# Two more attention steps get their sums over keys from a pair of fp16 matmuls instead of one fp32 matmul

## What is computed

```
attn = softmax(q k^T * scale)                 # over 666 keys
x = x + (attn v) @ Wout
x = x + sum_e score_e * (relu(LN(x) @ W1_e + b1_e) @ W2_e + b2_e)
```

## Time and profile before

| | us |
|---|---|
| runs | 343.05, 342.17, 342.32 |
| median | 342.32 |
| profiled execution | 342.39 |
| its span (first to last instruction) | 340.7 |
| PE busy | 331.6 (97%) |
| POOL busy | 287.5 (84%) |
| DVE busy | 274.1 (80%) |
| ACT busy | 214.5 (63%) |

### The profile page before, as it was taken

The page is one execution under the profiler, slowest core; times in us unless marked ns, Lnnn a source line. Parts: engine busy times, 40 slices in busy tenths (PEclk is TensorE's granted clock), DMA queues, the critical chain, the costliest instruction groups (busy, mean ns, idle before and its releaser), DMA issues.

```text
span 340.7 us, 5981 instructions
## 1 busy us (share of the span) xinstructions
PE 331.6 (97%) x2193; PEld 220.5 (65%) x2193; DVE 274.1 (80%) x416; ACT 214.5 (63%) x303; POOL 287.5 (84%) x186
## 2 busy tenths in 40 slices
PE   7899999999999999999999999999999999999993
PEld 7676666574847565665757474756694548888782
DVE  5988667988899899999988798979728786499476
ACT  2464668584948476675858494857622745587980
POOL 4629999999999999999999999999993999488540
PEclk9999999999999999999999999999999999999998
DMA  4640000000010000000000000000000007000611
GB/s 128 194 118 0 2 0 4 0 17 0 2 31 16 17 2 0 3 1 2 15 2 15 18 0 17 0 2 1 2 0 3 0 0 228 22 0 2 189 63 62
DMA packets 9049, 10.03 MB, mean 29 GB/s; under 512 B 1015, under 2 KB 6061, under 8 KB 9021
## 3 DMA queue, kind: packets, MB, share of 16 engines
q1 hardware_dynamic: 8725, 9.52, 9.3%
q10 hardware_dynamic: 296, 0.13, 0.1%
HBM read 9.09 MB, written 0.56 MB: 28 GB/s over the span
## 4 chain that ended last, share of the span: by engine, by line
PE 90%; ACT 3%; DVE 3%; POOL 1%; issue 1%; DMA 1%; ACTq 0%; DVEq 0%
PE xo L476 25%; PE sc L456 21%; PE sc L462 6%; PE sc L382 5%; PE sc L384 4%; PE sc L383 4%; PE mx L413 3%; PE xo L413 3%; PE mx L564 2%; PE xo L564 2%; PE xo L485 2%; PE mx L383 1%; PE mx L382 1%; PE mx L384 1%; POOL relu_lo L1275 1%
## 5 line engine op out<-in xcount | busy, mean ns | idle before, releaser
L1297 POOL TENSOR_TENSOR psum_acc<-psum_acc,probs 111x1024 f32<-111x1024 f32 x64 | 164.0, 2562 | 6.9
L768 ACT ACTIVATE probs<-sc 111x1024 f32<-111x1024 f32 x96 | 98.2, 1027 | 18.5 <-PE sc L462 11.9
L476 PE MATMUL xo<-probs,v_sb 111*64 111x512 f32 x384 | 88.0, 596 | 0.0
L456 PE MATMUL sc<-q_pair,k_pair 64*111 64x512 f32 x576 | 86.0, 402 | 0.8 <-ACT v_sb L758 0.4
L456 PEld LDWEIGHTS sc<-q_pair,k_pair 64*111 64x111 f32 x576 | 44.6, 171 | 28.4 <-issue 11.5
L995 DVE RECIPROCAL recips<-recips 128x128 f32<-128x128 f32 x64 | 54.0, 903 | 0.0
L476 PEld LDWEIGHTS xo<-probs,v_sb 111*64 111x64 f32 x384 | 26.3, 137 | 42.7 <-issue 39.4
L961 DVE TENSOR_REDUCE part_max<-mx 128x2 f32<-128x888 f32 x32 | 34.7, 1083 | 20.5 <-PE mx L413 19.0
L1297 POOL TENSOR_TENSOR psum_acc<-probs 111x1024 f32<-111x1024 f32 x16 | 39.3, 2458 | 7.8 <-ACT probs L768 7.6
L784 ACT COPY recips<-xo 128x512 f32<-128x512 f32 x16 | 9.4, 587 | 57.5 <-PE xo L485 48.8
L462 PE MATMUL sc<-max_row,ones_r 64*111 64x512 f32 x192 | 38.3, 390 | 0.0
(11 more groups left out here) (238 smaller groups left out, 619.8 us busy)
## 6 DMA issues: line engine op xcount, KB each, us to landing
spread<-score_rows SPq DMA_DIRECT2D x16, 256.0 KB, 5.7
w_raw<-in_L_ffn_W SPq DMA_DIRECT2D x8, 128.0 KB, 2.1
x_tok<-in_x SPq DMA_DIRECT2D x2, 256.0 KB, 3.2
wv_raw<-in_L_xattn_Wkv SPq DMA_DIRECT2D x4, 128.0 KB, 2.9
wout_sb<-in_L_xattn_Wout SPq DMA_DIRECT2D x1, 512.0 KB
wqk_raw<-in_L_xattn_Wq SPq DMA_DIRECT2D x7, 64.0 KB, 2.0
wqk_raw<-in_L_xattn_Wkv SPq DMA_DIRECT2D x7, 64.0 KB, 2.1
out<-x_tok SPq DMA_DIRECT2D x1, 256.0 KB, 2.0
```

The source lines that it names most:

```text
L456: pe.matmul(sc[0:KP, kt % 2, h, :], k_pair[r, s % QKB, k_part, at], q_pair[r, s % QKB, q_part, :], start=(k_part + q_part == 0), stop=False)
L476: mm = pe.matmul(o_ps[h * HD:(h + 1) * HD, :], v_sb[0:KP, s // 2 % 2, kt, at:at + HD], probs[0:KP, e % RING, h, :], start=(kt == 0), stop= ...
L768: act.activation(probs[0:KP, e % RING, :, :], sc[0:KP, kt % 2, :, :], ACT.Exp).then_inc(exp_done, 1)
L1297: pool.tensor_tensor(psum_acc[0:KP, s % 2, :, :], first, probs[0:KP, e % RING, :, :], ALU.add) \
```

## The change

`HALVED` goes from `STEPS - 3` to `STEPS - 1`, so `total(13)` and `total(14)` take the two fp16 parts too; `total(15)` stays fp32. The places of the `total` calls on PE are the same as before, which the rewritten condition keeps. ACT gets `sum_high(13)` behind the exponents of step 14 and `sum_high(14)` behind that step's last `w2_high`. DVE gets `sum_low(13)` as the last call of its loop, behind `spread_max(15)`, and `sum_low(14)` behind `norm_x1(0)`, ahead of the `reciprocal(12)` calls. The reciprocals keep their places. `gather(15, 1)` now waits on `acc_lo_done` in place of `sum_ready`.

```diff
-HALVED = STEPS - 3
+HALVED = STEPS - 1
@@ PE, step s
                 turn_max(s + 1)
-                if s > HALVED:
-                    total(s - 1)
                 for kt in range(KT):
-                    if kt == SUM_AT and 1 <= s <= HALVED:
+                    if kt == (SUM_AT if s < STEPS - 2 else 0) and s >= 1:
                         if s == 1:
                             pe.wait_ge(kv_ready, 3)
                         total(s - 1)
@@ ACT, step s
-                if 2 <= s <= HALVED:
+                if 2 <= s < STEPS - 1:
                     sum_high(s - 1)
@@
                 for e in W2_HI_AT.get(s, ()):
                     w2_high(e)
+                if s == STEPS - 2:
+                    sum_high(s)
@@ DVE, step s
-                if 1 <= s <= HALVED:
+                if s >= 1:
                     sum_low(s - 1)
-                if 2 <= s <= HALVED:
+                if 2 <= s < STEPS - 2:
                     for c in range(RC):
                         reciprocal(s - 2, c)
@@ DVE, behind the loop
             x1_and_moments(0, x1_ps[0])
             norm_x1(0)
+            sum_low(STEPS - 2)
             for c in range(RC):
                 reciprocal(STEPS - 4, c)
```

## The result

| | before | after |
|---|---|---|
| median, us | 342.99 (342.17 to 343.05, 5 runs) | 346.67 (346.42 to 347.23, 5 runs) |
| profiled execution | 342.39 | 346.42 |
| its span | 340.7 | 344.7 |

The ratio is 1.0121, 95% interval 1.0108 to 1.0135, which is 4.1 us (3.7 to 4.6). In the two profiled executions the difference is 4.03 us. The two medians lie only 3.7 us apart, since the runs of before are of two kinds, near 342.2 and near 343.0, and its median is one of the upper ones. The forecast was 345.3, that is +3.0; the rival in which the clock falls was put at 346.6.

The account below looks back on a forecast made before the run. PE, busy for 97% of the span, was taken to bound the kernel: +3.1 (stall) - 0.96 (two totals) + 0.9 (second wait) = +3.0 us, forecast 345.3 us, range 343.9 to 346.8.

Parts of the forecast that it names:

- the rival in which the clock falls: `pv(14)` runs partly at 1.2 GHz after the stall, 2.2 us added, PE +4.3: 346.6 us; chance 0.14.
- The stall: PE waits ahead of `total(13)` for `sum_low(13)`, which stands behind `spread_max(15)` on DVE: 3.1 us.
- The length of `sum_low`: `sum_low(13)` waits for the end of the `gather` under way, then takes 1.08 us, ending at 258.62.
- DVE's and POOL's lateness: Both `sum_low` calls delay `reciprocal(12)` by 3.26 us; POOL's row follows, its last `gather` ending at 282.55.
- The second wait: PE waits ahead of `total(15)` for POOL's late last `gather`: 0.9 us.
- The clock: Granted clock stays at 1.00 in `pv(14)` behind the stall; no time added.
- two totals: `total(13)` and `total(14)` on PE each get 0.48 us shorter in fp16: -0.96 us.

Follow-up runs that it names:

- ingap: Changed kernel with `sum_low(13)` moved ahead of `spread_max(15)` on DVE; ratio 1.006 to the kernel before, median 344.45 us.
- w2late: Changed kernel with POOL's `w2_low(0)` moved from ahead of step 14's last `gather` to behind `rstd_x1(0)`; ratio 1.0112 to before, median 346.49 us.
- awake: Changed kernel with 12 unread identity matmuls on PE between `turn_max(15)` and `total(13)`; ratio 1.0107 to the kernel before.
- ingap_awake: Changed kernel with `sum_low(13)` ahead of `spread_max(15)` and 7 unread identity matmuls ahead of `total(15)`; ratio 1.0028 to before, median 343.33 us.
- gap13_swap: Changed kernel with only `total(13)` split, `sum_low(13)` ahead of `spread_max(15)`, `bias_term(0)` ahead of `total(15)`; ratio 1.0013 to before, median 342.63 us.
- only13: Changed kernel with only `total(13)` split, `total(14)` left fp32; ratio 1.0135 to the kernel before, median 347.51 us.
- only14: Changed kernel with only `total(14)` split, `total(13)` left fp32; ratio 1.0062 to the kernel before, median 344.53 us.

## Why the prediction was right or wrong

**The stall: right.** Forecast: `sum_low(13)` from 256.43 to 258.62, `total(13)` at 258.8, `pv(14)` 2.6 us late. Measured: 256.46 to 258.66, 258.71, 2.57. That DVE's wide gap is of no use, since the call stands behind the instruction that PE releases last, is shown by ingap, where the stall is gone with that order alone.

**The length of `sum_low`: right.** It ends 1.08 to 1.09 us behind the end of the `gather`, at four places of it (kernel after, w2late, ingap, and the call in the earlier trace rows). The rule of the Trainium skill ("SBUF — State Buffer", section "Who interferes with whom") holds here: whoever begins first holds the interface for its whole instruction. In ingap it shows in the other direction too, in the `gather` of 3.15 us begun during `sum_low`.

**DVE's and POOL's lateness: right, but hidden.** `reciprocal(12)` came 3.28 us late (forecast 3.26). The second wait, put at 0.9 us, was 0.16 in the kernel after, since PE had lost 1.67 us elsewhere by then. With the clock kept up (awake) it was 0.75.

**The clock: wrong, and this is the step that failed.** The forecast had "the granted clock 1.00 in `pv(14)`" and gave the fall a chance of 0.14. The sum had no term for it. By profile or mean clock it fell in 9 of 9 runs of the changed kernel, and cost 1.67 us. It is the rival's mechanism, at 1.67 us on PE where I had taken 2.2. That its 346.6 is next to the measured 346.67 is in part luck: it stood for +4.3 on a median of 342.32, and the profiles say +4.0. The 346.67 lies inside my range only since the range had been stretched over this rival. Its size was a guess below a bound of 2.9 from the factor 1.55, and the factor was too small: in ingap matmuls of 128x512 start 0.43 us apart at a clock of 0.50, against 0.23 at 1.00. What kept the cost at 1.67 is that the low stretch lasted only 3.4 us.

My argument against the rival was that in the output stage the clock stayed at full through the 2.15 us gap. That was so, but what I took from it was wrong. The windows of the kernel before (columns as above):

```profile
336.00:337.00 1.00, 0.41 (x2) 0.20 (x2) 0.93 (x4) 0.00 (x0) 0.00 (x0) 1.00 0.00 0
```

With the earlier trace rows: the clock is still full at 336.59, where PE resumes, and fell at some 337.4, after it had resumed. The fall comes late, so a full clock inside a gap says nothing of what follows; only the rows behind the gap do, and these showed the 0.71. Nor was "dense before and behind" any protection in the changed kernel.

In terms of the sum: forecast +3.1 stall - 0.96 + 0.9 = +3.0; measured +3.00 stall - 0.88 (two totals) + 1.67 clock + 0.16 second wait + 0.05 = +4.00.

The Trainium skill ("TensorE: Matmul & The Clock Gate", section "Why this matters for your kernels") warns of idle gaps between bursts of matmuls. The runs agree, and for shorter gaps than I would have taken it to mean: 1.61 us of idleness was followed by the half clock in the profile of ingap, and with PE kept busy there (ingap_awake) it did not come.

## What to carry to other kernels

A gap of an engine is only usable for what stands, in that engine's order, ahead of the instruction that ends the gap: before giving an idle engine more work, look at which instruction of the waiting engine releases it, and whether the waiting engine's next one needs the new work. Where PE is dense, price each new wait of it over half a microsecond with a fall of the clock as well, here another 1.5 to 1.7 us as often as the table has it, and look for that behind the wait (0.3 to 2.1 us after PE resumed in the four profiles that show it) and not in it; where a wait can't be avoided, matmuls whose result nobody reads paid for themselves (1.1 us in ingap_awake). And when PE is made faster, find the row (here POOL's, whose last `gather` ended 0.39 us ahead of `total(15)`) that has been arriving just in time.

## What the runs showed of the hardware

The clock's fall doesn't take a certain length of wait: by profiles and mean clocks, after 2.8 to 2.9 us it came in 14 of 15 runs, after 1.1 us in four of six, after 0.65 us in a quarter. Runs of one kernel with and without it lie 1.5 to 2.6 us apart (gap13_swap 342.5 and 344.0, only13 344.9 and 347.5); a fall by itself cost 1.5 to 1.7 us in the profiles, and up to 1.0 can come from the start. A reader of one profile sees one draw: only13's and only14's profiles were the lucky ones, 2.6 and 1.3 us under their medians.
